# A two-layer cross-attention kernel: staged blocks get a longer allowance, queries are projected in one run per batch, dot products follow the transposes

## The reference, cut to what matters

```python
Q, K, V = (q @ Wq.T + bq), (k @ Wk.T + bk), (v @ Wv.T + bv)       # 16 heads of 32
att = softmax(einsum('bhqd,bhkd->bhqk', Q, K) / sqrt(32))
x1 = layernorm(einsum('bhqk,bhkd->bhqd', att, V) @ Wo.T + bo + q) * gamma0 + beta0
Q_phi, K_phi = elu(x1), elu(ctx)
KV = einsum('bnd,bne->bde', K_phi, ctx)
Z = 1.0 / (einsum('bnd,bd->bn', Q_phi, K_phi.sum(axis=1)) + 1e-6)
out = layernorm(x1 + einsum('bnd,bde->bne', Q_phi, KV) * Z) * gamma1 + beta1
```

## Time and profile before

| | |
|---|---|
| median of 3 runs | 1574.0 us (1573.15 to 1576.62) |
| the profiled execution's own time | 1583.65 us |
| its span | 1581.9 us |
| TensorE busy, granted clock | 1477.9 us (93%), 0.968 |
| VectorE, GpSimd, ScalarE busy | 1317.8, 1269.1, 932.3 us |
| DMA: moved, mean rate | 183.70 MB, 116 GB/s |
| copies of `w_parts<-w_dram` (512 KB) | 45 |

### The profile page before, as it was taken

One profiled execution on the slowest core, in us unless ns is written; L12 is line 12 of the kernel. 1 busy time (PEld: TensorE's weight loads), 2 busy tenths in 40 slices (PEclk: granted clock), 3 DMA queues, 4 the chain that ended last, 5 costly groups with the idle time before them and its releaser, 6 DMA issues.

```text
span 1581.9 us, 29154 instructions
## 1 busy us (share of the span) xinstructions
PE 1477.9 (93%) x9976; PEld 1015.8 (64%) x9976; DVE 1317.8 (83%) x2448; ACT 932.3 (59%) x1892; POOL 1269.1 (80%) x1069
## 2 busy tenths in 40 slices
PE   8998999999999999999999999999999898998986
PEld 5775776667757667566666767667665555555654
DVE  5768878887788898788999889987978889998874
ACT  3445555665666656556665656655756555665563
POOL 0457777777799988877988989987969899899863
PEclk9999999999999999899999999999999999999998
DMA  7646645246344515333552532445241221301000
GB/s 255 198 132 187 227 154 165 87 122 202 98 125 131 147 47 174 97 124 90 188 145 86 167 90 94 136 143 150 90 124 50 72 62 45 103 27 37 26 16 34
DMA packets 136754, 183.70 MB, mean 116 GB/s; under 512 B 19104, under 2 KB 69408, under 8 KB 136608
## 3 DMA queue, kind: packets, MB, share of 16 engines
q1 hardware_dynamic: 134352, 179.22, 37.4%
q10 hardware_dynamic: 2256, 2.63, 0.5%
HBM read 125.18 MB, written 56.62 MB: 115 GB/s over the span
## 4 chain that ended last, share of the span: by engine, by line
PE 53%; DVE 14%; POOL 13%; issue 10%; DMA 5%; ACT 3%; SPq 1%; POOLq 0%; DVEq 0%; ACTq 0%
PE acc L732 9%; PE score L697 9%; PE scoreT L711 9%; PE misc L790 7%; POOL pair_sum L1327 7%; DVE maxes L1071 5%; PE misc L786 4%; PE misc L827 4%; DVE pair_sum L1111 4%; PE misc L802 4%; PE misc L819 3%; DMA stage<-ctxT_in 1%; POOL pair_sum L1336 1%; PE acc L748 1%; ACT p_ring L894 1%
## 5 line engine op out<-in xcount | busy, mean ns | idle before, releaser
L894 ACT ACTIVATE p_ring<-scoreT 128x512 f32<-128x512 f32 x1024 | 595.8, 593 | 465.6 <-PE scoreT L711 459.5
L1071 DVE TENSOR_REDUCE maxes<-score 128x1 f32<-128x512 f32 x1024 | 672.2, 676 | 123.2 <-PE score L697 120.3
L1327 POOL TENSOR_TENSOR pair_sum<-p_ring 128x512 f32<-128x512 f32 x504 | 664.8, 1327 | 129.6 <-ACT p_ring L894 76.3
L697 PE MATMUL score<-k_stack,q_stack 96*128 96x512 f32 x1024 | 535.1, 523 | 36.4 <-DVE maxes L1071 34.2
L711 PEld LDWEIGHTS scoreT<-q_stack,k_stack 104*128 104x128 f32 x2048 | 388.0, 194 | 177.4 <-ACT p_ring L894 89.8
L711 PE MATMUL scoreT<-q_stack,k_stack 104*128 104x256 f32 x2048 | 430.9, 292 | 29.5 <-ACT p_ring L894 24.2
L697 PEld LDWEIGHTS score<-k_stack,q_stack 96*128 96x128 f32 x1024 | 196.0, 191 | 194.1 <-issue 88.7
L732 PE MATMUL acc<-p_ring,v_sb 128*32 128x256 f32 x4096 | 260.3, 397 | 0.0
L1111 DVE TENSOR_TENSOR pair_sum<-pair_sum 128x512 f32<-128x512 f32 x189 | 234.2, 1239 | 24.9 <-POOL pair_sum L1327 24.7
L1336 POOL TENSOR_TENSOR pair_sum<-pair_sum 128x512 f32<-128x512 f32 x189 | 254.7, 1347 | 0.0
L732 PEld LDWEIGHTS acc<-p_ring,v_sb 128*32 128x32 f32 x4096 | 123.6, 113 | 90.6 <-issue 11.3
(11 more groups left out here) (129 smaller groups left out, 1485.1 us busy)
## 6 DMA issues: line engine op xcount, KB each, us to landing
q_stack<-q_dram SPq DMA_DIRECT2D x189, 128.0 KB, 2.6
k_stack<-k_dram SPq DMA_DIRECT2D x93, 256.0 KB, 5.7
w_parts<-w_dram SPq DMA_DIRECT2D x45, 512.0 KB, 5.6
k_dram<-kept_parts SPq DMA_DIRECT2D x28, 512.0 KB, 3.1
q_dram<-kept_parts SPq DMA_DIRECT2D x27, 512.0 KB, 3.1
ctx_nat<-ctx_in SPq DMA_DIRECT2D x32, 256.0 KB, 3.7
v_sb<-v_dram SPq DMA_DIRECT2D x15, 512.0 KB, 4.3
tiles<-x_in SPq DMA_DIRECT2D x27, 256.0 KB, 3.5
```

Of the source, the lines that this page charges most:

```text
L697: pe.matmul(score[k % 3][:], q_stack[0:SPLIT, unit % NQ, j, t * P:(t + 1) * P], k_stack[0:SPLIT, group_of[unit] % 2 * QUAD + j, h * HALF:( ...
L894: act.activation(p_ring[:, n % NP, h * HALF:(h + 1) * HALF], scoreT[k % 2][:], ACT.Exp, scale=SCALE).then_inc(A["exped"], 1)
L1071: dve.reduce_max(maxes[:, unit % 2, t, j, h:h + 1], score[k % 3][:], AX.X).then_inc(V["maxed"], 1)
L1327: pool.tensor_tensor(pair_sum[:, place_of_pair(pair), cols], p_ring[:, (n - 1) % NP, cols], p_ring[:, n % NP, cols], ALU.add).then_inc(L[" ...
```

## The change

- `load_stage` allows 5 steps instead of 3 between a load and its split, from step `UT * UB + UT` = 272 on.
- In batches 2 and 3 the second halves of the four query projections come right behind the first halves; before, they came last in their batch. The `earliest` steps of late projections are 10 apart instead of 9.5, and their deadline is 36 steps behind instead of 56.
- `dot` waits for the tile's transposes and writes its products over the tile's features; the planner books it two steps or more behind `T`, no longer behind `phi`, and `A` may not start before it. The tile `unused` is gone.
- `outT` has 21 places instead of 19.
- `put_kept` is booked one step later, and DVE's cost of a projection's end is booked one step later. In DVE's own program `keep_low` stays where it was, in the step in which the projection ends (both lookups read `ended.get(k)`).
- A new constant `SHORT` lets some units sum three pairs instead of four. It is set to `UNITS - 1`, as `SUMMED` is, so that every unit has the pairs it had; `pairs_of`, `lows_until`, `highs_until`, `add_last` and the new form of `place_of_pair` then give the same numbers, waits and instructions as before. They are left out of the diff, but for the first two lines.

```diff
-    NQ, NP, NO, NX = 3, 7, 19, 3
+    NQ, NP, NO, NX = 3, 7, 21, 3
     EXACT = 4
     NPHI = 3
     VISIT = 4
     VISITS = KT * UNITS // VISIT
-    RUN_PAIRS = KT // 2
-    RUNS = RUN_PAIRS - 1
+    SLOTS = KT // 2
     SUMMED = UNITS - 1
+    SHORT = UNITS - 1
...
+    def pairs_of(unit):
+
+        return SLOTS if unit < SHORT else SLOTS - 1 if unit < SUMMED else 0
...
-        projections += [*(("Q", g, cp) for cp in range(2 if b == 1 else 1) for g in groups), *(("V", b, kb) for kb in blocks),
+        projections += [*(("Q", g, cp) for cp in range(2) for g in groups), *(("V", b, kb) for kb in blocks),
                         *(("K", g, 0) for g in groups), *(("K", g, 1) for g in groups),
-                        *(("V", b, kb + KT // 2) for kb in blocks), *(("Q", g, 1) for g in groups if b > 1)]
+                        *(("V", b, kb + KT // 2) for kb in blocks)]
...
-        unused = sb("unused", [P, D])
...
-                return FIRST if n < 3 * UB // 2 else 280 + 19 * (n - 3 * UB // 2) // 2
+                return FIRST if n < 3 * UB // 2 else 280 + 10 * (n - 3 * UB // 2)
...
-                return earliest(kind, i) + 56 if earliest(kind, i) > FIRST else FIRST
+                return earliest(kind, i) + 36 if earliest(kind, i) > FIRST else FIRST
...
-            return use, k + 3
+            return use, k + (3 if k < UT * UB + UT else 5)
...
-            phi_of[i] = book("phi", "DVE", max(grow_of[i], end_of.get(("T", i - 1), FIRST), dot_of.get(i - 1, FIRST)) + 1, 10, i)
-            dot_of[i] = book("dot", "DVE", phi_of[i] + 1, 13, i)
+            phi_of[i] = book("phi", "DVE", max(grow_of[i], end_of.get(("T", i - 1), FIRST)) + 1, 10, i)
...
-            take("DVE", end, cost[1])
+            take("DVE", end + (kind == "P"), cost[1])
...
-                    put = send("put_kept", end + 1, turn_of_kept[what], 2, False)
+                    put = send("put_kept", end + 2, turn_of_kept[what], 2, False)
...
+                dot_of[i] = book("dot", "DVE", end + 2, 13, i)
...
+                if kind == "A" and k < dot_of.get(i, LATE):
+                    return False
...
-                dve.wait_ge(V["phi_made"], tile + 1)
+                dve.wait_ge(T["phi_turned"], tile + 1)
                 dve.wait_ge(A["ksum_kept"], tile // KT + 1)
                 dve.tensor_tensor_reduce(
-                    out=unused[:], in0=x_nat[slot_of[tile]], in1=phi_total[:], scale=1.0, scalar=0.0,
+                    out=x_nat[slot_of[tile]], in0=x_nat[slot_of[tile]], in1=phi_total[:], scale=1.0, scalar=0.0,
...
-                if kind == "P" and projections[number_of][0] in "KQ":
+                earlier, at = ended.get(k, (None, 0))
+                if earlier == "P" and at > 1 and projections[at][0] in "KQ":
+                    keep_low(at)
+                if kind == "P" and number_of < 2:
```

More of the change, by code:

```diff
@@ L52, in half_of, with pairs_until, lows_until, highs_until @@
         return i // (QUAD * TPC), i // TPC % QUAD, i % TPC
-    def place_of_pair(pair):
-        unit, p = divmod(pair, RUN_PAIRS)
+    def pairs_of(unit):
+        return SLOTS if unit < SHORT else SLOTS - 1 if unit < SUMMED else 0
+    def pairs_until(unit):
+        return sum(pairs_of(u) for u in range(unit))
+    def lows_until(unit):
+        return pairs_until(unit) - unit
+    def highs_until(unit):
+        return sum(pairs_of(u) - 1 if u < SHORT else 1 for u in range(unit))
+    def place_of_pair(unit, p):
         return unit % 2 if p == 0 else 1 - unit % 2
@@ L325, in build @@
             take("ACT", k + LEAD, 6)
-            if k // 2 % 2 == 0 and k < UT * SUMMED:
+            p = k % UT // 4
+            if k // 2 % 2 == 0 and p < pairs_of(k // UT):
                 take("POOL", k + LEAD + 4, 13)
-            if k % 4 == 0 and k % UT > 0 and k < UT * SUMMED:
+            if k % 4 == 0 and 0 < p < pairs_of(k // UT):
                 take("POOL", k + LEAD + 6, 13)
-                take("DVE", k + LEAD + 7, 10)
+                take(*(("POOL", k + LEAD + 7, 13) if p == 2 and k >= UT * SHORT else ("DVE", k + LEAD + 7, 10)))
             if k % UT < 4:
@@ L1105, in add_high @@
             def add_high(unit, p):
-                whole, part = (pair_sum[:, place_of_pair(RUN_PAIRS * unit + i), HALF:2 * HALF] for i in (0, p))
-                dve.wait_ge(L["paired"], 2 * (RUN_PAIRS * unit + p + 1))
+                whole, part = (pair_sum[:, place_of_pair(unit, i), HALF:2 * HALF] for i in (0, p))
+                dve.wait_ge(L["paired"], 2 * (pairs_until(unit) + p + 1))
                 if p > 1:
-                    dve.wait_ge(V["run_high"], RUNS * unit + p - 1)
+                    dve.wait_ge(V["run_high"], highs_until(unit) + p - 1)
                 dve.tensor_tensor(whole, whole, part, ALU.add).then_inc(V["run_high"], 1)
@@ L1304, in vector_program @@
                     make_phi(when["phi"][k])
-                pair, i = divmod(k - LEAD - 7, 4)
-                unit, p = divmod(pair, RUN_PAIRS)
-                if 0 <= unit < SUMMED and p > 0 and i == 0:
+                slot, i = divmod(k - LEAD - 7, 4)
+                unit, p = divmod(slot, SLOTS)
+                if 0 <= unit < SUMMED and 0 < p < (pairs_of(unit) if unit < SHORT else 2) and i == 0:
                     add_high(unit, p)
@@ L1328, in add_pair @@
                                    p_ring[:, n % NP, cols], ALU.add).then_inc(L["paired"], 1)
             def add_low(unit, p):
-                whole, part = (pair_sum[:, place_of_pair(RUN_PAIRS * unit + i), 0:HALF] for i in (0, p))
-                pool.wait_ge(L["paired"], 2 * (RUN_PAIRS * unit + p) + 1)
+                whole, part = (pair_sum[:, place_of_pair(unit, i), 0:HALF] for i in (0, p))
+                pool.wait_ge(L["paired"], 2 * (pairs_until(unit) + p) + 1)
                 if p > 1:
-                    pool.wait_ge(L["run_low"], RUNS * unit + p - 1)
+                    pool.wait_ge(L["run_low"], lows_until(unit) + p - 1)
@@ L1336, in add_low, with add_last @@
                 pool.tensor_tensor(whole, whole, part, ALU.add).then_inc(L["run_low"], 1)
+            def add_last(unit):
+                whole, part = (pair_sum[:, place_of_pair(unit, p), HALF:2 * HALF] for p in (0, 2))
+                pool.wait_ge(L["paired"], 2 * pairs_until(unit + 1))
+                pool.wait_ge(V["run_high"], highs_until(unit + 1))
+                pool.tensor_tensor(whole, whole, part, ALU.add).then_inc(L["run_last"], 1)
             def add_bias(tile):
@@ L1420, in gpsimd_program @@
                     shift1(when["shift1"][k])
-                pair, i = divmod(k - LEAD - 4, 4)
-                if 0 <= pair < RUN_PAIRS * SUMMED and i < 2:
-                    add_pair(pair, i)
-                unit, p = divmod(pair, RUN_PAIRS)
-                if 0 <= unit < SUMMED and p > 0 and i == 2:
-                    add_low(unit, p)
+                slot, i = divmod(k - LEAD - 4, 4)
+                unit, p = divmod(slot, SLOTS)
+                if 0 <= unit < SUMMED and p < pairs_of(unit):
+                    if i < 2:
+                        add_pair(unit, p, i)
+                    elif i == 2 and p > 0:
+                        add_low(unit, p)
+                    elif i == 3 and p == 2 and unit >= SHORT:
+                        add_last(unit)
         def sync_program():
```

39 lines of the change are left out of this document (23 added, 16 removed).

## The result

| | before | changed |
|---|---|---|
| median (4 runs each) | 1574.29 us | 1595.98 us (1594.61 to 1598.99) |
| ratio, 95% interval | | 1.0135 (1.0117 to 1.0153) |
| profiled execution: own time, span | 1583.65, 1581.9 us | 1595.76, 1594.1 us |
| granted clock | 0.968 | 0.964 |

The kernel became 21.7 us slower, where I forecast 3.5 faster with 1581 as the far end. The two profiles differ by only 12.2 us, because the one of before lay 9.65 above its median.

The account below looks back on a forecast made before the run. Three engines near their limit (TensorE 93%, VectorE 83%, GpSimd 80%) leave only PE's idle time and lost clock to win. Gains of -10.85 and costs of +7.4 make -3.5: median 1574.0 to 1570.5 us, 8-in-10 range 1559 to 1581.

Parts of the forecast that it names:

- The kept buffer, place 2: Step 728: store goes out 5.1 us behind `keep_high`, ACT waits 3.7 us for it: +2.3 us, bounds 0 and +5.5.
- place 3: Queries' second halves: stores no longer behind `stack_queries` and context loads, where ACT waited 3.82 us: -2.3 us, bounds 0 and -3.4.
- Staging elsewhere: ACT's waits for staged blocks from step 272 on, outside the context's stretch: -1.4 and -1.8 us, bounds 0 and -5.4.
- Dot product: `dot`, now between transposes and attention, still hides under a visit's 2 us of PE: 0, within 2 us either way.
- Longer bare stretches: Bare steps stand together as `A` starts later behind `T`, and clock is lost: +1.7 us, between 0 and +8.5.
- Place 1, staging there: Third batch's context blocks: both ACT waits go, -3.65 us, and the clocks' difference, -1.7 us; bounds 0 and -5.35.
- The second batch's store: Group 4's second-half store goes out behind loads and `stack_queries`; ACT waits 3.6 us: +1.5 us, bounds 0 and +3.6.
- Stores behind `put_max`: Steps 130, 210, 450 and 690: store behind `put_max`, 0.8 us of ACT's wait each: +1.9 us, bounds 0 and +4.8.
- Values: Third batch's values, load booked at step 542 for a visit at 551, arrive in time: 0, at worst +3 us.
- The stores decide: Rival: PE pays ACT's wait in full where stores queue behind other DMAs: slower, 1578.7 us; chance 0.16.
- The clock decides: Rival: some ten units between steps 786 and 982 lose clock in longer bare runs: slower, 1577.3 us; chance 0.12.

## Why the prediction was wrong

**The kept buffer, place 2: the step that failed.** "Lands at 8.2, and ACT waits 8.2 - 4.5 = 3.7 us" added the median landing of 3.1 us to an issue 5.1 us behind `keep_high`. The issue was right (4.66). The landing was 9.4. I counted the six DMAs ahead by the 2.75 us that SP needs to issue them and forgot that their 1.5 MB must be moved (1.8 MB were issued and had not landed). ACT waited 9.56 us, beyond my bound of 5.5, PE showed 8.11 of it, and the half clock behind it came on top. The number was in rows I had quoted: at place 3 the store was issued at 1146.35 behind 1 MB of context loads and ACT was freed at 1152.4. The trace of before on that one DMA:

```profile
DMA to landing us min/median/max: 6.0/6.0/6.0
```

I took 3.1 for the new place and had 6.0 from the old. The traces of before, of the changed kernel and of the first eleven experiments together (715 stores), by the bytes issued and not yet landed when the store is issued: nothing in flight, 3.0 us median; 0.3 to 0.6 MB, 3.4; 0.6 to 1.1 MB, 4.1; 1.1 to 1.6 MB, 5.9; 1.6 to 2.1 MB, 7.0 (thirteen stores); beyond, 9.9 (two stores). The Trainium skill ("DMA: Bandwidth & Descriptors", section "Queues, rings and completion order") says that each DMA engine takes a queue's descriptors in ring order. These landings agree with it.

**Staging elsewhere, the second failure.** "The last 1.8 go" held for the context but not for the last queries' blocks: 0.7 + 2.8 us of ACT, which made POOL wait 4.2 and cost steps 544 to 576 about 5 us. ACT's waits for `stage` fell to 3.9 us, not under 2. For the same reason: I compared an allowance of five steps with old waits, not with what is in flight at the new place (1.8 and 2.9 MB issued and not yet landed when the two blocks are issued).

**Dot product: a term of 0 that was not.** I priced it "0, within 2 either way" as if only its own length counted. What its turn changes is where `dot` and `phi` stand against POOL's runs. By two differences of ratios that costs 0.3 to 0.5%, not clear of noise, and the 6.38 us wait of PE at step 569 is of this kind. The later stores I gave no term of their own beside those behind `put_max`; they cost 0.6 to 0.7%, and how is open.

**Longer bare stretches: sized at the wrong end.** I wrote "The total of bare steps is unchanged, but they stand together" and priced their clock, +1.7. The pieces that left such steps stand elsewhere, in steps 448 to 512 and 736 to 768, where PE hardly waits, so that every piece adds its time: these are 8.3 and 3.9 us longer in the changed kernel, and no term had them.

**Place 1, staging there: right.** No wait for `ctxT_in` is left in the list, and the clock of steps 416 to 448 rose from 0.90 to 1.00 and their time fell from 49.2 to 45.0 us. Alone, the allowance gave 6 us of the 8.55 forecast. **Place 3: right** in the main: 3.82 us of ACT's wait are now 1.31 (the store went behind six DMAs of `stack_keys`, and only the five steps to the next projection saved it). **The second batch's store:** ACT waited 2.55 us, for my 3.6. **Stores behind `put_max`:** ACT waited 1.48, 1.50, 1.48 and 1.53 us at the four, for my 0.8; undersized. **Values:** no wait, as said.

**The rivals.** "The stores decide" had the right mechanism at one place but, with the same 3.1 us of landing in it, the wrong price: 8.2 us above the forecast, where the result lies 25.5 above. "The clock decides" did not come: steps 786 to 982 took 277.1 us at 0.96 before and 279.4 at 0.95 now, 2.3 us for my 1.7:

```profile
1175.50:1454.90 279.40, 253.93 (x1696) 161.25 (x1694) 258.61 (x472) 170.94 (x363) 256.60 (x220) 0.95 0.22 62
```

No rival named a DVE operation held up by POOL. What stays open: how the later stores cost, how often the long operations occur, and how much a table would win that spreads the pieces as before.

## What to carry to other kernels

Price a store or load at a new place by the bytes in flight ahead of it at its issue, not by the median of the page, and check each transfer that is moved past for how early it is really needed. Where two transfers compete, send first the one that somebody waits for within a few steps, and let the bulk that is needed 36 steps later go behind it. In a written-out order a step of one is a change of neighbours: test the parts of such a change alone before keeping it, since here one part gained 6 us and was buried under the others. And where work moves, price the stretch that gets it as well as the one that loses it: here the steps with slack gave nothing back, and those without it took all.

## What the hardware showed that I had not expected

An operation of DVE with two inputs in SBUF can wait out a whole run of POOL's operations: 8.4 to 8.5 us under seven, 6.8 under six, 6.0 under five, 4.3 to 5.5 under four, 4.2 under three, and in every such case of all sixteen profiles it ends 0.55 us behind the last of them. The trace of before had seven operations of 4.2 to 5.5 us, so this could have been read there. The row maxima, which read PSUM, never do:

```profile
L1095 DVE TENSOR_REDUCE maxes<-score x1024: 632/677/693, 27.8 to 1513.5; 128x1 f32<-128x512 f32 x171
```

The Trainium skill ("SBUF — State Buffer", section "Summary: rules for kernel authors") describes the conflict between DVE and GpSimd and says that the second to issue blocks until the first finishes. The kind of operation agrees; the length does not, since DVE waited through six further operations of POOL, all of which began after it, and here the measurement decides.
